# Routing places and shares moved behind the last head, pairs sent a turn later, context centred behind its load, its transpose split behind the key stacks

## The reference

```python
def reference(x, ctx_2048, ...):                    # 16 batches, S=256, D=512, float32
    x = _layernorm(x + _L0_attn_ref(x, ...))        # attention: 16 query heads, 4 key heads of 32, rope on half a head
    x = _layernorm(x + _L0_xattn_ref(x, ctx_2048, ctx_2048, ...))
    x = _layernorm(x + _L0_ffn_ref(x, ...))
    return x

def _mlstm_forward(q, k, v, Wi, bi, Wf, bf, ln_scale):       # 16 heads of 32; k = v = ctx_2048
    x = jnp.concatenate([q, k, v], axis=-1)
    ig = (x @ Wi + bi)...; fg = (x @ Wf + bf)...
    ...
    log_D = log_fg + jnp.transpose(ig, (0, 1, 3, 2))
    max_log_D = jnp.max(log_D, axis=-1, keepdims=True)
    D = jnp.exp(log_D - max_log_D)
    qk = jnp.einsum('bhsd,bhtd->bhst', qh, kh) / jnp.sqrt(jnp.asarray(dh, q.dtype))
    C = qk * D
    normalizer = jnp.maximum(jnp.abs(C.sum(-1, keepdims=True)), jnp.exp(-max_log_D))
    h = jnp.einsum('bhst,bhtd->bhsd', C / (normalizer + EPS), vh)
    mu = h.mean(-1, keepdims=True)
    var = ((h - mu) ** 2).mean(-1, keepdims=True)
    return ((h - mu) * jax.lax.rsqrt(var + EPS) * ln_scale)...

def _L0_ffn_ref(x, router_w, router_bias, Wu, Wg, Wd, Su, Sg, Sd):    # 16 experts, top 2, one shared expert
    logits = flat @ router_w.T
    _, topk_idx = jax.lax.top_k(logits + router_bias, TOPK)
    topk_scores = softmax(logits)[topk_idx] / (their sum)
    for e in range(N_EXPERTS):
        out = out + combine[:, e:e + 1] * ((_silu(flat @ Wu[e]) * (flat @ Wg[e])) @ Wd[e])
    ...                                             # plus the shared expert, of width 512
```

## Time and profile before

| | us |
|---|---|
| median of 3 runs | 2085.5 (2080.51 to 2090.78) |
| the profiled execution | 2090.95 |
| its span | 2089.3 |
| TensorE busy in it | 1871.2 (90%) |
| VectorE busy | 1196.6 (57%) |
| ScalarE busy | 650.3 (31%) |
| GpSimd busy | 696.2 (33%) |
| mean granted TensorE clock | 0.951 |

### The profile page before, as it was taken

The page is one execution under the profiler, slowest core; times in us unless marked ns, Lnnn a source line. Parts: engine busy times, 40 slices in busy tenths (PEclk is TensorE's granted clock), DMA queues, the critical chain, the costliest instruction groups (busy, mean ns, idle before and its releaser), DMA issues. The chain is left out here.

```text
span 2089.3 us, 35576 instructions
## 1 busy us (share of the span) xinstructions
PE 1871.2 (90%) x11010; PEld 1185.8 (57%) x11011; DVE 1196.6 (57%) x2474; ACT 650.3 (31%) x1358; POOL 696.2 (33%) x754
## 2 busy tenths in 40 slices
PE   3879999999999999999999999998879999999990
PEld 2456575766657576665757666575644444444440
DVE  2567777766776776677777667776442222222225
ACT  1142433334243333424333342433302212222224
POOL 3124133332413333241333324133123444444430
PEclk8789999999999999999999999999979999999995
DMA  7153242344424234441423444142324666656549
GB/s 274 44 124 98 56 118 72 90 110 89 118 42 118 72 88 111 89 118 42 118 72 89 111 89 118 41 99 62 105 102 87 134 168 163 148 121 142 90 77 334
DMA packets 151843, 226.92 MB, mean 109 GB/s; under 512 B 32448, under 2 KB 107200, under 8 KB 149056
## 3 DMA queue, kind: packets, MB, share of 16 engines
q1 hardware_dynamic: 101616, 132.94, 24.6%
q0 software_dynamic: 38336, 92.38, 18.4%
q10 hardware_dynamic: 11792, 0.61, 0.4%
HBM read 94.70 MB, written 48.83 MB: 69 GB/s over the span
## 5 line engine op out<-in xcount | busy, mean ns | idle before, releaser
L1575 PE MATMUL ps<-ug_w,rowsT 128*128 x640 | 292.8, 601 | 8.1 <-SPq L1424 4.5
L1575 PEld LDWEIGHTS ps<-ug_w,rowsT 128*128 128x128 f32 x640 | 123.0, 193 | 163.7 <-issue 163.7
L1464 POOL DMA_INDIRECT sum_rows<-y_sb,pairs x80 | 127.3, 1591 | 248.6 <-DVE y_sb L1542 136.5
L869 DVE RECIPROCAL arden<-ps 128x256 f32<-128x256 f32 x64 | 112.5, 1758 | 140.2 <-PE ps L1321 136.6
L1064 PE MATMUL ps<-wqkv_sb,xT_sb 128*128 128x256 f32 (+1 forms) x512 | 172.3, 490 | 15.3 <-ACT maskr_sb L524 15.3
L1530 DVE SCALAR_TENSOR_TENSOR silu<-tanh,ps 128x256 f32<-128x256 f32 x80 | 33.7, 422 | 251.7 <-ACT tanh L1485 251.7
L961 DVE SCALAR_TENSOR_TENSOR weighted<-ps,decay 128x384 f32<-128x384 f32 x256 | 139.2, 553 | 66.4 <-PE ps L1190 50.4
L851 DVE TENSOR_REDUCE smax<-ps 128x2 f32<-128x512 f32 x256 | 164.0, 682 | 16.5 <-PE ps L1247 16.5
L476 POOL DMA_INDIRECT routed_ids<-pair_w,pos_w x64 | 64.0, 1000 | 324.7 <-DVE pair_w L747 288.1
L641 ACT ACTIVATE probs<-ps 128x1024 f32<-128x1024 f32 x128 | 130.8, 1024 | 114.8 <-PE ps L1298 114.8
L620 ACT ACTIVATE decay<-ps,g_col 128x256 f32<-128x256 f32 x256 | 121.3, 474 | 137.5 <-PE ps L1173 90.8
(11 more groups left out here) (253 smaller groups left out, 3835.0 us busy)
## 6 DMA issues: line engine op xcount, KB each, us to landing
q_stack<-qkT_hi SPq DMA_DIRECT2D x128, 128.0 KB, 3.8
mk_stack<-ctxT_hi SPq DMA_DIRECT2D x128, 128.0 KB, 5.1
mq_stack<-qkT_hi SPq DMA_DIRECT2D x128, 128.0 KB, 2.4
ug_w<-in_expert_ug SPq DMA_DIRECT2D x16, 1024.0 KB, 5.3
xT_sb<-in_xT SPq DMA_DIRECT2D x16, 512.0 KB, 3.3
x_sb<-in_x POOLq DMA_DIRECT2D x16, 512.0 KB, 3.8
ctxT_sb<-in_ctxT POOLq DMA_DIRECT2D x16, 512.0 KB, 3.6
q_stack<-qkT_lo SPq DMA_DIRECT2D x64, 128.0 KB, 4.3
```

The source lines that it names most:

```text
L1464: pool.indirect_dma_start(out=sum_dram, out_offset=bass.IndirectOffsetOnAxis(ap=tables.pairs[:, m, 0:1], axis=0), in_=y_sb[:, m % W, :], i ...
L1575: ins = nc.tensor.matmul(ps[:, 2 + k % 2, :], rowsT[:, k % 2, c, :], ug_w[:, bass.ds(slot, 1), c, :].rearrange("p o n -> p (o n)"), start= ...
```

## The change

1. `place_rows` moves behind the last head, `place_shares` behind `average(1)`, `exp_gap` behind `square` in the second pair of the attention exponentials.
2. The pairs of w are sent one turn later, behind the split; `body(2)` is unrolled on GpSimd and its loop runs from 3.
3. `centre` moves from the top of the next turn to right behind its load, ahead of the power on the head variances.
4. The split of the transposed context moves behind the DMAs of the key stack.
5. Buffers: `scored` and `ranks` get their own; `hid` and `sq` become one, and `qk_sb` is laid over it, for which ScalarE waits for x2 of batch w before it writes q and k; the gate weights are 64 instead of 128 columns wide.

```diff
-        gw_hi = sb("gw_hi", [P, 2 * KC, P], F32R)
-        gw_lo = sb("gw_lo", [P, 2 * KC, P], F32R)
+        gw_hi = sb("gw_hi", [P, 2 * KC, 2 * GR], F32R)
+        gw_lo = sb("gw_lo", [P, 2 * KC, 2 * GR], F32R)
...
-        qk_sb = sb("qk_sb", [P, ST, QKH, HD])
...
-        hid = sb("hid", [P, ST, H, HD])
-        sq = sb("sq", [P, ST, H, HD])
+        hid_sq = sb("hid_sq", [P, 2, ST * H * HD])
+        hid, sq = (hid_sq[:, q, :].rearrange("p (t h d) -> p t h d", h=H, d=HD) for q in range(2))
+        qk_sb = hid_sq[:, :, :].rearrange("p a n -> p (a n)")[:, 2 * QKH * ROT:2 * QKH * ROT + ST * QKH * HD]\
+            .rearrange("p (t h d) -> p t h d", h=QKH, d=HD)
...
-        scored, ranks = (hid_flat[:, ST * H * HD - q * TOPK * ST * E:ST * H * HD - (q - 1) * TOPK * ST * E]
-                         .rearrange("p (k t e) -> p k t e", k=TOPK, e=E) for q in (1, 2))
+        scored, ranks = sb("scored", [P, TOPK, ST, E]), sb("ranks", [P, TOPK, ST, E])
...
             def body(b, y, w, more):
-                if y is not None:
-                    centre(y)
-                if b is not None:
+                def split_context():
...
+                if b is not None:
                     wait(pool, t_ready, b, 0)
                     wait(pool, qk_lo_done, b, 2, rest=rest)
                     stack(pool, k_stack, qkT_hi, qkT_lo, KC, k_in, K_ROWS)
-
-                if w is not None:
-                    wait(pool, pairs_done, w, 1, rest=rest)
+                    split_context()
+
+                def send_pairs(v):
+                    wait(pool, pairs_done, v, 1, rest=rest)
...
+                if w is not None and not (isinstance(w, int) and w == 0):
+                    send_pairs(w - 1)
+                if b is None and y is None:
+                    send_pairs(w)
...
                     pool.dma_start(ctx_sb[:, :, :, :].rearrange("p t h d -> p t (h d)"), one(ctx_v, b)).then_inc(ctx_row_in.sem, 16)
+                    centre(b)
...
+                        if w is not None:
+                            wait(act, x2_done, w, ST)
...
-                        if h == SHARES_AT - 2 and w is not None:
-                            exp_gap()
...
                         if i == 1 and y is not None:
                             take_hid(1)
                             square()
+                            if w is not None:
+                                exp_gap()
...
-                            if w is not None and h == PLACES_AT:
-                                place_rows()
-                            if w is not None and h == SHARES_AT:
-                                place_shares()
...
+                        if w is not None:
+                            place_rows()
+                            if b is None:
+                                place_shares()
...
                         average(1)
+                        if w is not None:
+                            place_shares()
                         average(2)
```

More of the change, by code:

```diff
@@ L247, in attention_and_mlstm @@
         gw_raw = weighted_flat[:, 0:6 * KC * H].rearrange("p (k g h) -> p k g h", g=2, h=H)
-        gw_f = hT[:, :, :].rearrange("p c (a n) -> p (c a) n", n=P)
+        gw_f = hT[:, 0:2, :].rearrange("p c (a n) -> p (c a) n", n=2 * GR)
         ps = ctx.enter_context(nc.psum_tensor("ps", [P, 8, 512], F32))
@@ L320, in attention_and_mlstm @@
         FIRST_NUM, FIRST_HID = 10, 13
-        RANKS_AT, PLACES_AT, SHARES_AT = 1, 3, 9
+        RANKS_AT = 1
         def scored_beside(h):
@@ L511, in _ @@
             body(1, 0, None, True)
+            body(2, 1, 0, True)
             pool.wait_ge(ids_clear.sem, 4 * 16)
-            with pool.Fori(2, B - 1) as i:
+            with pool.Fori(3, B - 1) as i:
                 body(i, i - 1, i - 2, True)
@@ L1077, in gate_mm @@
                             for wt, v in ((gw_hi, hi), (gw_lo, hi), (gw_hi, lo)):
-                                ins = nc.tensor.matmul(ps[:, 5, 0:S], wt[:, KC * side + c, :], v[:, c, :],
+                                ins = nc.tensor.matmul(ps[0:2 * GR, 5, 0:S], wt[:, KC * side + c, :], v[:, c, :],
                                                        start=n == 0, stop=n == 6 * KC - 1)
```

## The result

The changed kernel took 2167.16 us (median of 4 runs, 2162.93 to 2168.37) against 2088.14 us for the kernel before: ratio 1.0367, 95% interval 1.0308 to 1.0425. The forecast was slower, 2128 us, range to 2145 us; the loss is 79 us, nearly twice the 42.6 us of the sum.

A forecast was written before the change was run, and what follows sets the result against it. TensorE was taken to bound the kernel. Own turns, (-1.0 + 1.9 + 2.0) x 14 = 40.6 us, plus 2.0 us for turn 1, made 42.6 us slower: 2128 us against the 2085.5 us median, range 2064 to 2145 us.

The forecast's parts named there:

- Part 1, the loop: Head loop: taking places and shares out shortens it from 19.98 to 19.0 us, a gain of 1.0 us a turn.
- Part 1, the cover: Behind the last head: places cost nothing while VectorE waits for the first reciprocal; 2.8 us if that cover were gone.
- Part 2: Gate operations and x1 scaling: moving split and centring frees some 2.8 us of VectorE and more, worth nothing to TensorE.
- Part 3: Split behind key stacks: GpSimd holds VectorE's last gate operations, first decay matmul 1.9 us late a turn; bounds 0 and 1.9.
- Part 4: Centring behind its load: holds VectorE's variance steps, second average late; bounds 1.1 and 2.9 us a turn, taken 2.0.
- its second half: Behind the second average: GpSimd's power on the variances holds the share sum, ending the averages 2.9 us late.
- Part 5: The rest: pairs sent a turn later, narrower gate weights and the q/k overlay on the hidden buffer each change nothing.
- Clock: Granted clock, 0.97 over eight turns, costs at most 22 us there; allowed 10 us either way, counted nothing.

The follow-up runs named there:

- load_late: sends_top with the context load issued behind the second layernorm's power instead of behind the last value matmul: 2076.99 us, ratio 0.9793.
- jump_first: Changed kernel with the places at the top of the second half of VectorE's turn, behind its loop's jump: 2142.22 us, ratio 1.0234.
- routing_back: Changed kernel with places, shares and gap exponential back in the head loop and pairs sent in their own turn: 2157.56 us, ratio 1.0191.
- centre_back: Changed kernel with the context centred at the top of the next turn again, the load staying: 2147.92 us, ratio 1.0148.
- best_split: sends_top plus the edit of jump_first, with the split put behind the key stacks again: 2121.28 us, ratio 1.0023.
- route_only: Changed kernel with the edits of split_back and centre_back together: 2157.01 us, ratio 1.0174.
- split_back: Changed kernel with the split of the transposed context ahead of the key stack DMAs again: 2171.63 us, ratio 1.0252.
- sends_top: route_only with the pairs of the turn before sent at the top of GpSimd's turn instead of behind the key stacks: 2121.36 us, ratio 1.0124.

## Why the prediction was wrong

**Part 1, the loop: right.** I priced 1.0 us a turn, 14 us; it gave 18.1 us (303.5 to 285.4), because in four turns of the kernel before the loop took 21.0 to 21.9 us.

**Part 1, the cover: the step that failed.** "The places go behind the last head, where VectorE has nothing until the first reciprocal, which waited 7.3 us for TensorE in this turn: I cost them at nothing there." The 7.3 us were no free room. VectorE's jump lay in them: the branch at 782.4, the next instruction of the sequencer at 785.2, and the load issued only at 784.77. 2.9 us of places pushed the branch behind the issue, and the jump then took 6.4 to 8.4 us; without the load it would have been 4.0 us, and places and jump together would just have fitted. The first average cost 16.9 us, and its lateness is part of the second's. load_late (0), jump_first (0), routing_back (0) and the on-time turns show it; centre_back shows that GpSimd's operations have no part. That VectorE waits for instructions is as good as shown: its sequencer starts nothing, two packets of the instruction queue fall into each gap, and 54 of the 77 are gone where the gap is gone; only that the queue is VectorE's is inferred. The Trainium skill ("Runtime: NRT & Kernel Launch", section "Instruction fetch mechanics") states this mechanism: fetching ahead is sequential only, and a taken branch to a page that is not held stalls the engine until a DMA has brought it. The two packets in each gap agree. I did not look for the loop's cut when I looked for cover.

**Part 2: right.** The scaling of x1 takes 1.00 us for 2.31, L929 0.27 for 2.43, and in turns 2 to 13 TensorE gained nothing from either. It had waited for the scaling in turns 1, 14 and 15, 5.8 us in all, and still waits 3.5 us in one.

**Part 3: right, 1.9 us forecast, 2.2 measured** (31.0 us in 15 turns), two operations earlier than I had it. By itself it costs more than its wait: 40 us in best_split, 26 of them idle time and 14 busy time at a lower clock.

**Part 4: its size was right, its second half wrong.** Alone it is 1.4 us a turn (bounds 1.1 to 2.9, taken 2.0). The share sum is not held: L755, with two SBUF inputs, takes at most 0.16 us inside the power, in all 15 turns. The Trainium skill ("SBUF — State Buffer", section "SBUF: two separate sides"), by which it would be held, has the measurement against it here. The held L955 and L956 have one SBUF input each, which that section allows for in a fast mode alone; no row here shows an operation's mode.

**Part 5: "Nothing" for the pairs was right by luck.** In the changed kernel the sends, 3.3 us into the turn, stop nobody. Moved up by 5 us they cost 41 us in 15 turns, and back in their own turn, in routing_back, 9 us.

**Clock: mis-sized.** I allowed 10 us and counted nothing; it is 20.9 us of busy time for the same matmuls. Right behind the 2.69 us wait (windows):

```profile
731.00:734.00 3.00, 2.90 (x28) 1.64 (x32) 2.87 (x5) 0.74 (x1) 1.75 (x1) 0.71 0.01 3
```

a mean of 0.71, which is the 2.4 GHz level for part of the stretch and the 1.2 GHz level for the rest.

The sum as it came out, over 15 turns: gate rows +30.2, second average +22.4, first average +16.9, busy time at a lower clock +20.9, less 14.0 of idle time saved, half of it in the loop (6.9): 76.4 us. The forecast had the first two, the last, and nothing for the other two, 37.8 us together.

## What to carry to other kernels

Idle time of an engine is cover only as far as nothing invisible is in it: look up where its hardware loop jumps and how long the sequencer's rows stand still there, and keep that point ahead of large transfers or put the moved work behind it. An edit beside the jump can also change how much the loop fetches: compare the instruction packets. When two stalls end at the same place, undoing one shows nothing; undo both, then put each back alone. A wait also costs what the matmuls behind it run slower by.

## What the runs showed of the hardware

A jump of VectorE's loop took 4.0 us from its branch to the sequencer's next instruction with two instruction packets in the gap, and 6.4 to 9.1 us with the context load in flight as well; 2.7 to 3.6 us with one packet; 0.3 us with none. Only with the load did it last longer than the idle time that the places left. GpSimd's split held VectorE's operations with one SBUF input (1.52 us for 0.27), its power of 5.46 us held none. Four indirect sends in a row delayed what ScalarE and VectorE wait for from TensorE until 1 us behind the last of them (1.2 to 1.5 us behind the matmuls), in route_only, split_back and routing_back, less in centre_back, and not in the kernel before, the changed one or sends_top.
